# A selective-scan stage whose front products use two PSUM banks in turn, with two decay banks in place of three

## What is computed

```python
x_and_res = inputs @ W_in
x, res = jnp.split(x_and_res, 2, axis=-1)
x = silu(depthwise_conv_same(x, K_conv, b_conv))
A = -jnp.exp(A_log)
x_dbl = inputs @ W_x
delta, Bm, Cm = jnp.split(x_dbl, [DT_RANK, DT_RANK + D_STATE], axis=-1)
delta = softplus(delta @ W_dt + b_dt)
deltaA = exp(delta * A);  deltaB_u = delta * x * Bm      # 256 channels, 16 states
h = deltaA_t * h + deltaB_u_t;  y_t = sum over states of h * C_t
y = (y + x * D) * silu(res)
return y @ W_out + b_out
```

## Time and profile before

| what | us |
|---|---|
| median of three runs (1678.16 to 1689.12) | 1682.97 |
| profiled execution | 1677.74 |
| its span, first to last instruction | 1675.6 |
| TensorE busy | 1433.5 (86%) |
| VectorE busy | 1171.5 (70%) |
| ScalarE busy | 521.5 (31%) |
| GpSimd busy | 528.3 (32%) |
| mean granted clock of TensorE | 0.92 of full |

### The profile page before, as it was taken

The page is one execution under the profiler, slowest core; times in us unless marked ns, Lnnn a source line. Parts: engine busy times, 40 slices in busy tenths (PEclk is TensorE's granted clock), DMA queues, the critical chain, the costliest instruction groups (busy, mean ns, idle before and its releaser), DMA issues.

```text
span 1675.6 us, 21605 instructions
## 1 busy us (share of the span) xinstructions
PE 1433.5 (86%) x7414; PEld 1056.8 (63%) x7414; DVE 1171.5 (70%) x2649; ACT 521.5 (31%) x1011; POOL 528.3 (32%) x448
## 2 busy tenths in 40 slices
PE   3996877795999999985878878878887599999998
PEld 2893545695899999972333333333333389999996
DVE  3666763575676677642798999999999656777753
ACT  2203444200122222213545455355454022222221
POOL 1130000000000000001788888888899100000000
PEclk9997997797999999986889989999998799999998
DMA  4000000001433333201232323332322233333330
GB/s 134 2 1 1 1 1 1 1 1 55 148 102 102 102 102 102 102 1 33 84 90 79 97 68 94 93 79 84 101 84 86 80 124 108 108 109 108 108 108 13
DMA packets 74154, 121.30 MB, mean 72 GB/s; under 512 B 9591, under 2 KB 18750, under 8 KB 73918
## 3 DMA queue, kind: packets, MB, share of 16 engines
q1 hardware_dynamic: 74046, 119.93, 22.9%
HBM read 116.75 MB, written 3.15 MB: 72 GB/s over the span
## 4 chain that ended last, share of the span: by engine, by line
PE 68%; DVE 17%; issue 8%; POOL 4%; ACT 2%; DMA 1%; DVEq 0%; POOLq 0%; ACTq 0%
PE bank L1083 21%; PE bank L1086 7%; PE bank L1201 7%; PE bank L940 5%; PE bank L1145 3%; DVE xe L1567 2%; PE bank L976 2%; DVE both L1559 2%; PE bank L1043 2%; DVE hs L1567 2%; PE bank L1028 2%; POOL both L578 2%; PE bank L1095 2%; PE bank L1025 2%; PE bank L985 1%
## 5 line engine op out<-in xcount | busy, mean ns | idle before, releaser
L1083 PE MATMUL bank<-wqkv_sb,xe 128*128 128x192 f32 x2048 | 369.4, 333 | 10.0 <-DVE xe L1503 9.9
L1083 PEld LDWEIGHTS bank<-wqkv_sb,xe 128*128 128x128 f32 x2048 | 339.1, 194 | 21.4 <-DVE xe L1503 14.9
L1201 PE MATMUL bank<-both,ident 128*128 128x512 f32 x512 | 267.6, 651 | 17.8 <-DVE both L1559 16.8
L546 POOL TENSOR_TENSOR rstd<-ve,half_neg 128x4 f32<-128x4 f32 x32 | 37.5, 1173 | 748.4 <-DVE ve L1254 748.4
L824 ACT ACTIVATE bank<-dt,A 128x512 f32<-128x512 f32 x256 | 172.7, 685 | 167.8 <-DVE xe L1567 93.3
L1201 PEld LDWEIGHTS bank<-both,ident 128*128 128x128 f32 x512 | 104.8, 211 | 151.9 <-issue 108.1
L578 POOL TENSOR_TENSOR both<-du,prob 128x512 f32<-128x512 f32 x128 | 161.0, 1269 | 34.8 <-DVE xe L1567 20.1
L578 POOL TENSOR_TENSOR both<-du,prT 128x512 f32<-128x512 f32 x128 | 160.6, 1269 | 15.3 <-DVE hs L1567 10.7
L1567 DVE TENSOR_TENSOR_SCAN hs<-bank,both 128x512 f32<-128x512 f32 x128 | 153.3, 1208 | 0.0
L1567 DVE TENSOR_TENSOR_SCAN xe<-bank,both 128x512 f32<-128x512 f32 x128 | 152.5, 1208 | 0.0
L940 PEld LDWEIGHTS bank<-exp_sb,xe 128*128 128x128 f32 x1024 | 138.5, 197 | 5.0
(11 more groups left out here) (272 smaller groups left out, 2061.2 us busy)
## 6 DMA issues: line engine op xcount, KB each, us to landing
dt<-w_rows SPq DMA_DIRECT2D x128, 256.0 KB, 4.1
du<-w_rows SPq DMA_DIRECT2D x128, 256.0 KB, 5.0
prob<-bc_dram SPq DMA_DIRECT2D x64, 256.0 KB, 3.3
prT<-bc_dram SPq DMA_DIRECT2D x64, 256.0 KB, 3.3
at<-bc_dram SPq DMA_DIRECT2D x20, 256.0 KB, 3.3
qk_sb<-bc_dram SPq DMA_DIRECT2D x20, 256.0 KB, 3.3
xs<-in_x_dram SPq DMA_DIRECT2D x8, 256.0 KB, 3.8
out_dram<-xs SPq DMA_DIRECT2D x8, 256.0 KB, 2.4
```

The source lines that it names most:

```text
L546: pool.tensor_tensor(rstd[:], ve[:], half_neg[:, 0:NT], ALU.pow).then_inc(ln_rstd, 1)
L1083: m = pe.matmul(bank[4 + j // 2][:, (j % 2) * 3 * HD:(j % 2 + 1) * 3 * HD], x_e, wqkv_sb[:, e, :], start=(e == 0 and j % 2 == 0), stop=(e ...
L1201: pe.matmul(bank[4 + k % NH][:], ident[:], hc[k % HRING], start=False, stop=(SUM_RANK[k] == sums_of(k // UNITS, k % NH))).then_inc(hc_used, 1)
```

## The change

The eleven front products alternate between bank 7 and bank 2 (`FRONT_IN`), each waiting only for the last reader of what stood before it in its own bank. Bank 2 is taken from the decays: they have banks 0 and 6, and the decay of unit U+1 is emitted at clock U. Because `th`, `lz` and `thr` are single buffers in SBUF that the single bank used to guard as well, ScalarE now waits for their last reader by name.

```diff
@@ plan
 DRING = 6
 FRONT7 = {"xT": -8, "rows": -6, "conv0": -4, "dlt": 0, "bcT": 2, "conv1": 8, "z0": 12, "z1": 16, "res0": 20, "res1": 22}
 OUT7 = 6
+FRONT_IN = {"xT": 7, "rows": 2, "conv0": 7, "dlt": 2, "bcT": 7, "conv1": 2, "z0": 7, "z1": 2, "res0": 7, "res1": 2, "out": 7}
...
-BEFORE7 = {TURNS[i + 1][1:]: TURNS[i][1:] for i in range(len(TURNS) - 1)}
+BEFORE7 = {}
+for i in (2, 7):
+    there = [turn[1:] for turn in TURNS if FRONT_IN[turn[1]] == i]
+    BEFORE7.update(zip(there[1:], there))
...
-        decay = [bank[0], bank[6], bank[2]]
+        decay = [bank[0], bank[6]]
+        front_bank = {name: bank[i] for name, i in FRONT_IN.items()}
...
@@ ScalarE
                     def tanh_u(h):
                         act.wait_ge(bank7_ps, seen(IN7[f"conv{h}", b]))
-                        act.activation(th[:], bank[7][:], ACT.Tanh, scale=0.5).then_inc(th_made, 1)
+                        act.wait_ge(u_made, seen(NH * b + h))
+                        act.activation(th[:], front_bank[f"conv{h}"][:], ACT.Tanh, scale=0.5).then_inc(th_made, 1)
...
                         act.wait_ge(ez_made, seen(n + 2))
+                        act.wait_ge(dt_made, seen(NH * b + h))
                         act.activation(lz[:], ez[:], ACT.Ln, bias=1.0).then_inc(ln_made, 1)
...
                         act.wait_ge(bank7_ps, seen(IN7[f"res{h}", b]))
-                        act.activation(thr[:], bank[7][:], ACT.Tanh, scale=0.5).then_inc(thr_made, 1)
+                        act.wait_ge(g_made, seen(NH * b + h))
+                        act.activation(thr[:], front_bank[f"res{h}"][:], ACT.Tanh, scale=0.5).then_inc(thr_made, 1)
...
                 for U in SCAN_CLOCK:
-                    if 0 <= U + 2 < ALL:
-                        decay_of(U + 2)
+                    if 0 <= U + 1 < ALL:
+                        decay_of(U + 1)
                     due(steps, U)
...
@@ TensorE
                     into_bank7("dlt", b)
-                    pe.matmul(bank[7][0:W3, :], wx_sb[:], xpad[:, 1:L + 1], start=True, stop=True).then_inc(bank7_ps, 1)
+                    pe.matmul(front_bank["dlt"][0:W3, :], wx_sb[:], xpad[:, 1:L + 1], start=True, stop=True).then_inc(bank7_ps, 1)
...
@@ VectorE
-                        dve.scalar_tensor_tensor(u2[par][:, h, :], th[:], 1.0, bank[7][:], ALU.add, ALU.mult).then_inc(u_made, 1)
+                        dve.scalar_tensor_tensor(u2[par][:, h, :], th[:], 1.0, front_bank[f"conv{h}"][:], ALU.add, ALU.mult).then_inc(u_made, 1)
...
```

More of the change, by code:

```diff
@@ L1137, in front @@
                     for j in range(NT):
-                        m = pe.matmul(bank[7][:, j * 32:(j + 1) * 32], xpad[:, 1 + j * P:1 + (j + 1) * P], wx_sb[:, DR:DR + 32], start=True, stop=True)
+                        m = pe.matmul(front_bank["rows"][:, j * 32:(j + 1) * 32], xpad[:, 1 + j * P:1 + (j + 1) * P], wx_sb[:, DR:DR + 32], start=True, stop=True)
                     m.then_inc(bank7_ps, 1)
@@ L1156, in front @@
                     into_bank7("bcT", b)
-                    rows = bank[7][0:W3, 0:L // 2].bitcast(BF16)
+                    rows = front_bank["bcT"][0:W3, 0:L // 2].bitcast(BF16)
                     for j in range(NT):
@@ L1164, in front @@
                         into_bank7(f"z{h}", b)
-                        pe.matmul(bank[7][:], wdt_sb[:, h * P:(h + 1) * P], dlt[:], start=True, stop=True).then_inc(bank7_ps, 1)
+                        pe.matmul(front_bank[f"z{h}"][:], wdt_sb[:, h * P:(h + 1) * P], dlt[:], start=True, stop=True).then_inc(bank7_ps, 1)
                         yield
@@ L1168, in front @@
                         into_bank7(f"res{h}", b)
-                        pe.matmul(bank[7][:], win_sb[:, DI + h * P:DI + (h + 1) * P], xpad[:, 1:L + 1], start=True, stop=True).then_inc(bank7_ps, 1)
+                        pe.matmul(front_bank[f"res{h}"][:], win_sb[:, DI + h * P:DI + (h + 1) * P], xpad[:, 1:L + 1], start=True, stop=True).then_inc(bank7_ps, 1)
                         yield
@@ L1173, in back @@
                     into_bank7("out", b)
-                    pe.matmul(bank[7][:], ones3[:, 0:P], bout3[:], start=True, stop=False)
+                    pe.matmul(front_bank["out"][:], ones3[:, 0:P], bout3[:], start=True, stop=False)
                     for h in range(NH):
@@ L1177, in back @@
                         for j in range(NT):
-                            m = pe.matmul(bank[7][:, j * P:(j + 1) * P], yg[:, h, j * P:(j + 1) * P], wout_sb[:, h, :],
+                            m = pe.matmul(front_bank["out"][:, j * P:(j + 1) * P], yg[:, h, j * P:(j + 1) * P], wout_sb[:, h, :],
                                           start=False, stop=(h == NH - 1 and j == NT - 1))
@@ L1515, in front @@
                     dve.wait_ge(bank7_ps, seen(IN7["rows", b]))
-                    dve.tensor_copy(bc_f[:], bank[7][:, 0:NT * 32].rearrange("p (j e) -> p j e", e=32)).then_inc(rows_read, 1)
+                    dve.tensor_copy(bc_f[:], front_bank["rows"][:, 0:NT * 32].rearrange("p (j e) -> p j e", e=32)).then_inc(rows_read, 1)
                     dve.wait_ge(rows_read, seen(b + 1))
@@ L1537, in front @@
                         dve.wait_ge(thr_made, seen(NH * b + h + 1))
-                        dve.scalar_tensor_tensor(g2[par][:, h, :], thr[:], 1.0, bank[7][:], ALU.add, ALU.mult).then_inc(g_made, 1)
+                        dve.scalar_tensor_tensor(g2[par][:, h, :], thr[:], 1.0, front_bank[f"res{h}"][:], ALU.add, ALU.mult).then_inc(g_made, 1)
                         yield
@@ L1549, in back @@
                     dve.wait_ge(acc_ps, seen(NB + b + 1))
-                    dve.tensor_tensor(seq(b), seq(b), bank[7][:], ALU.add).then_inc(acc_used, 1)
+                    dve.tensor_tensor(seq(b), seq(b), front_bank["out"][:], ALU.add).then_inc(acc_used, 1)
                     yield
```

18 lines of the change are left out of this document (9 added, 9 removed).

## The result

The changed kernel takes **1687.24 us** (median of 8, 1683.23 to 1692.24) where the kernel before takes 1683.14 (median of 8 run beside it, 1678.16 to 1689.12). The measured ratio is 1.0036, 95% interval 1.0019 to 1.0053: inside the 1% that I had called no change, a little on the slow side, and the interval leaves 1 out. The profiled execution has a span of 1685.2 us against 1675.6.

A forecast was written before the change was run, and what follows sets the result against it. VectorE was taken to bound the scan stage, with TensorE's throughput counting from the end of `yg` to `u`. The terms -10 - 1.7 + 10.2 + 5.2 = +3.7 us gave 1684 us, range 1669 to 1700.

The forecast's parts named there:

- 1% that I had called no change: Whole kernel: 1% (17 us) taken as what a measurement tells from no change; within 1% was given 81%.
- The start: Scan stage's start, first front: the second bank takes away waits on the path to the first scans, 10 us less.
- The short waits: Three short VectorE waits, where TensorE is late because `res1` had to wait for `g`: 1.7 us less, at least 0.
- The clock: TensorE before `skip_u`: 4.8 us idle in one piece lowers its clock afterwards, 1.7 us in six sequences, 10.2 us more.
- 2 or 3: Sign at the C product in every sequence: VectorE's wait grows from 1.02 to 2 or 3 us.
- The wait at `u`: VectorE at the second `u`, behind `th`: the wait keeps its 2.45 us, since both ends move with TensorE.
- The decays: ScalarE at the table load: unit 15's decay makes its scan 0.87 us late in six sequences, 5.2 us more.
- DMA and GpSimd: GpSimd and DMA queues keep their order; B and C rows leave 2 us earlier and were not waited for.
- The sum: All terms together: -10 - 1.7 + 10.2 + 5.2 = +3.7 us, no change that can be measured.
- the clock holds: Rival, ahead of `skip_u`: no gap is long, so the 10.2 us fall away; 1674 us, chance 22%.
- ScalarE falls behind everywhere: Rival: no spare decay, so front steps on ScalarE delay three places in six sequences; +17.8, 1698 us, chance 14%.
- the waits of 2.45 and 1.02 go: Rival: TensorE stays 3 us ahead through `skip_u`, so six times 3.47 us fall away; 1653 us, chance 9%.

The follow-up runs named there:

- fifth run: Kernel before, with the second bank for the first sequence's front only; later fronts stay in bank 7, decays keep three banks: 1669.29 us, ratio 0.9925.
- filler: Changed kernel plus four float32 matmuls nobody reads, between `bcT` and the second convolution from the second front on: 1677.45 us, ratio 0.9973 against the kernel before.
- dlt_waits: Changed kernel with one wait given back: `dlt` waits for the first `u` again, all banks as changed: 1676.13 us, ratio 0.9967 against the kernel before.
- sixth run: Changed kernel with the decay of unit 15 issued ahead of `az`, for every front but the first: 1685.46 us, ratio 1.0023 against the kernel before.
- decays_only: Kernel before with two decay banks and the decay of unit U+1 at clock U; the front stays in bank 7: 1694.15 us, ratio 1.0068.
- fourth kernel: Changed kernel with the second convolution (`conv1`) moved from clocks 8 and 10 to 3 and 4, directly behind `bcT`: 1653.03 us, ratio 0.9827 against the kernel before.
- eighth run: Changed kernel plus two unread matmuls in place of four, between `bcT` and the second convolution: 1684.92 us, ratio 1.0015 against the kernel before.

## Why the prediction came out right, and where its terms were off

- **The start**: -10, ends 7 and 13; measured -12.8 in the change and -12.4 in the fifth run, where it stands alone. The mechanism is as told, the size was low, and the term that fell short is the 1 us for the clock: the second convolution of the first front takes 3.70 us for 5.40 and the first one of the next front 5.82 for 6.74, 2.6 us in these two alone, while the first of all takes 0.2 more. The other half of the 2.8 us was not taken apart. From the second `u` to the second `g`, where I had left out the wait of the first `thr`, it is 4.8 us less for the 4.6 of my sum, so nothing of that wait shows.
- **The short waits**: -1.7; all gone, 2.4 with the two at `g` (0.7) that the earlier trace rows leaves out. What that bought was lost again at the split of the rows, below.
- **The clock**: +10.2, ends 0 and 13.8; the waits rose by 14.1, just over the upper end. The gap was forecast at 4.8 us and is 4.89 in five sequences of six and 4.25 in the other, `skip_u` takes the 2.04 of the earlier trace rows in the five, and the wait at C is 1.89 to 2.22, a little under the "2 or 3" that I had named as a sign, with the rest at `out`. The term was sized from the last sequence, whose waits of 1.33 and 1.89 give 2.2; those at `out` are now 1.92, 0.43, 2.36, 0.57, 2.36 and 0.60, with 1.89 to 2.22 at C. The sequences that wait 1.92 and 2.36 have the low rate on all of `out` (3.78 us), the others do not (2.05). I took 1.7 where that row gave 2.2, the mean is 2.3: my discount from the nearest row was the error. Runs 1 and 2, which undo the gap by two different means, give back 0.63 and 0.69% of the time, 11 to 12 us.
- **The wait at `u`** keeps its 2.45 to the hundredth, as both its ends move with TensorE.
- **The decays**: +5.2; measured 6 x 0.79 = 4.7 as waits. (My 0.87 was a slip: 1093.47 less 1092.63 is 0.84.) But taking them away in the sixth run returned about 2 us, within the noise of nothing or of 4.7, and the third shows that two banks alone cost 11 to 13 us with the front in one bank. As a term in this sum it was right; as the price of a lost bank it was not, since in the third run the low clock reached `skip_u` with it.
- **DMA and GpSimd**: nothing, I said. The queues did keep their order, but an effect of GpSimd on VectorE was missing from the sum, 2.7 us. VectorE splits the B and C rows into three bf16 parts (five instructions, L1279 to L1283, then L1287 to L1291). Over six sequences these take 25.2 us before and 27.8 in the change. By sequence, before: 3.70, 3.70, 4.25, and three times 4.51. The first three are just those with a short wait at a product, 0.72, 0.56 and 0.40 us, each 4.3 us ahead of the split. In the change that wait is gone, and the split takes 5.33 in the first sequence and 4.5 in each of the others. The runs `filler` and `dlt_waits`, also without short waits, have 27.0 in all. Without the wait the split stands earlier against GpSimd's products and has more of them beside it (the last section shows a pair), so most of what the short waits gave was lost within 10 us of them. That GpSimd's products are the cause is read from the timelines; no run took it apart.
- **The sum**: +3.7 forecast; the stage shows +6.7, the ratio +6.1, the medians +4.1. Errors of -2.8 and -0.7 at the start and the short waits and -0.5 at the decays stand against +3.9 at the clock and +2.7 at the split. That the total is near has some luck in it, as errors of 3 to 4 us were on both sides. So has the 1687 that the sum gives on the base of 1683.0, against 1687.24 measured.

Of the rivals, "the clock holds" is what the first two runs made of the kernel by hand: ratio 0.9973 and 0.9967, so some 10 us, the size it was given. That ScalarE falls behind everywhere did not happen in the change, but did in part in `decays_only`, at up to two places more a sequence. That the waits of 2.45 and 1.02 go was put at 1653 us, and needed another move than this change makes: with the convolution in the gap the fourth kernel measures 1653.03. That the two numbers agree is chance: this kernel keeps its waits of 1.02 at C and loses those for the decay, the rival had it the other way round.

The granted clock behind the gap is 0.50 from the first `skip_u` in five of the six sequences (4.89 us of standing), and from the second one in the sixth (4.25). The rule of the Trainium skill, "TensorE: Matmul & The Clock Gate", section "HAM oscillation — how this bites in real kernels", that a burst behind a long idle wait restarts at half rate every time round the loop, agrees with the five and comes one product late in the other. The same section of the Trainium skill reports of another kernel that a second PSUM buffer brought no further gain. At this kernel's start it is worth 12.4 us (fifth run); in the sequences behind it no run shows a gain from the bank by itself.

## What to carry to other kernels

When a wait is taken off an engine that is not the bound, ask where its idle time goes: two short pieces can become one long one directly ahead of the stretch where that engine does bound, and here TensorE then ran that stretch at half its clock (granted 0.50 behind 4.89 us). Look for such a piece in the timeline by its brackets, and move work that is ready into it, rather than put a wait back. A second buffer pays where nothing covers the wait (here the first front alone, 0.9925), so give it there and keep it for its former user elsewhere, or make a later step early by it.

## What the runs showed of the hardware that I had not expected

A small instruction of VectorE took four times as long beside GpSimd. Timelines of VectorE, of the kernel before and of the change:

```profile
926.20 0.29 DVE L1282 TENSOR_TENSOR bc_r<-bc_r,bc 128x128 f32<-128x128 f32 x1
```

```profile
1122.76 1.25 DVE L1290 TENSOR_TENSOR bc_r<-bc_r,bc 128x128 f32<-128x128 f32 x1
```

GpSimd's timelines beside them, in the same order:

```profile
923.54 2.54 POOL L578 TENSOR_TENSOR both<-du,prob 128x512 f32<-128x512 f32 x2
```

```profile
1121.32 2.54 POOL L583 TENSOR_TENSOR both<-du,prob 128x512 f32<-128x512 f32 x2
```

The subtraction takes 0.29 us at 926.20, when GpSimd's pair has ended at 926.08, and 1.25 at 1122.76, when it runs to 1123.86. Most of the slow instructions take close to one product of GpSimd (1.27 us); the longest, a conversion at 846.86 in the change, took 4.29 and spans three of them. The Trainium skill, "SBUF — State Buffer", section "SBUF: two separate sides", says that the two engines share a pair of ports under a lock held for a whole instruction, and that it takes a VectorE instruction in a fast mode or with two inputs in SBUF to want it. The rows agree: 1.25 for 0.29, and the scans beside the same products, with one input in PSUM, keep their 1.22.

The other is that the same gap does not always bring the same low clock. Two sequences of one kernel with the same 3.17 us gap had the rate fall in one and not in the other (eighth run), and behind 4.89 us `out` ran at the low rate in two sequences of the change and at the full one in three. Between the one profiled execution of the change and that of the sixth run the waits behind the gap went from 20.1 to 26.7 us, with VectorE's program shifted by 0.8 us a sequence and TensorE's untouched. Nor does the length of the gap alone decide: twelve `skip_u` pairs kept the full rate with up to 2.44 us of standing before them (second run), one lost part of it behind 1.45 us (first run), and in the change TensorE stands 3.01 us at 1126.04 and goes on at a granted clock of 1.00. What does decide stays open.
